# One of sixteen scan states weighted by C in transposed form on TensorE and ScalarE, and one more product with B on GpSimd, in an f32 selective-scan kernel

## The reference

```python
def step(h, inp):
    dt_t, B_t, C_t, x_t = inp
    dA = jnp.exp(dt_t[..., None] * A)
    dBx = dt_t[..., None] * B_t[:, None, :] * x_t[..., None]
    h = dA * h + dBx
    y = jnp.einsum('bdn,bn->bd', h, C_t)
    return (h, y)
...
return jnp.swapaxes(ys, 0, 1) + xc * D
```

## Time and profile before

| | |
|---|---|
| median of 3 runs | 16064.77 us (16052.41 to 16081.05) |
| the profiled execution | 16048.2 us, its span 16046.4 us |
| the gate's instructions, first to last | 2441.8 to 15980.0 us |
| busy share of the span | PE 88%, DVE 87%, POOL 81%, ACT 63% |
| granted TensorE clock | 0.932 of 2.4 GHz on the mean |

### The profile page before, as it was taken

The page is one execution under the profiler, slowest core; times in us unless marked ns, Lnnn a source line. Parts: engine busy times, 40 slices in busy tenths (PEclk is TensorE's granted clock), DMA queues, the critical chain, the costliest instruction groups (busy, mean ns, idle before and its releaser), DMA issues. The chain is left out here.

```text
span 16046.4 us, 144617 instructions
## 1 busy us (share of the span) xinstructions
PE 14080.0 (88%) x40704; PEld 5374.8 (33%) x40704; DVE 13972.3 (87%) x13537; ACT 10107.4 (63%) x14054; POOL 13048.9 (81%) x5650
## 2 busy tenths in 40 slices
PE   9999988888888888888888888888888888888887
PEld 3333333333333333333333333333333333333332
DVE  2222229999999999999999999999999999999998
ACT  2222226666666666766767667666666677666766
POOL 0000008999999999999999999999999999999997
PEclk9999998999999999999999999999999999999998
DMA  2111104444444545445455444554545454544545
GB/s 57 39 45 41 39 26 168 162 170 169 167 180 173 182 168 184 177 176 179 174 182 181 173 181 172 181 179 172 179 174 182 169 184 175 178 174 177 184 173 198
DMA packets 560175, 2505.16 MB, mean 156 GB/s; under 512 B 58919, under 2 KB 170879, under 8 KB 293264
## 3 DMA queue, kind: packets, MB, share of 16 engines
q1 hardware_dynamic: 548744, 2477.26, 43.7%
q10 hardware_dynamic: 10632, 18.65, 0.4%
HBM read 2325.11 MB, written 170.57 MB: 156 GB/s over the span
## 5 line engine op out<-in xcount | busy, mean ns | idle before, releaser
L811 POOL TENSOR_TENSOR hc<-h,c_all 128x1024 f32<-128x1024 f32 x4096 | 9526.8, 2358 | 490.3 <-DVE h L1178 460.5
L1048 PE MATMUL y_ps<-hc,ident 128*128 128x512 f32 x16392 | 8334.5, 660 | 1120.2 <-POOL hc L811 1119.9
L909 ACT ACTIVATE d_a<-dt,a_neg 128x512 f32<-128x512 f32 x8194 | 5598.2, 689 | 4045.1 <-DVE h L1178 4018.6
L1178 DVE TENSOR_TENSOR_SCAN h<-d_a,h,dbx_v 128x512 f32<-128x512 f32 x5456 | 6628.1, 1265 | 10.4 <-DVE dbx_v L1165 0.6
L1048 PEld LDWEIGHTS y_ps<-hc,ident 128*128 128x128 f32 x16392 | 3340.3, 210 | 6021.9 <-issue 4129.2
L1165 DVE TENSOR_TENSOR dbx_v<-dtx_ps,b_all 128x1024 f32<-128x1024 f32 x2816 | 3319.6, 1210 | 60.1 <-issue 25.2
L1178 DVE TENSOR_TENSOR_SCAN h<-d_a,h,dbx_p 128x512 f32<-128x512 f32 x2480 | 3029.4, 1263 | 10.4 <-issue 0.4
L800 POOL TENSOR_TENSOR dbx_p<-dtx,b_all 128x1024 f32<-128x1024 f32 x1280 | 3000.2, 2354 | 24.3 <-DVE h L1178 0.8
L495 POOL MEMSET ident_f<- 128x128 f32 x1 | 0.2, 204 | 2349.6 <-POOLq L46 2349.6
L289 PE MATMUL conv_ps<-image,w_taps 128*32 128x512 f32 x11520 | 1776.2, 594 | 0.0
L378 DVE RECIPROCAL k_inv<-k_nrm 128x4 f32<-128x4 f32 x256 | 45.5, 178 | 1750.0 <-ACT k_nrm L231 1750.0
(11 more groups left out here) (146 smaller groups left out, 9192.3 us busy)
## 6 DMA issues: line engine op xcount, KB each, us to landing
b_all<-bc_dram SPq DMA_DIRECT2D x1028, 1024.0 KB, 6.5
c_all<-bc_dram SPq DMA_DIRECT2D x1025, 1024.0 KB, 5.0
o_dram<-o_sb SPq DMA_DIRECT2D x257, 256.0 KB, 6.2
o_c<-o_dram SPq DMA_DIRECT2D x220, 256.0 KB
out<-r_c SPq DMA_DIRECT2D x220, 256.0 KB, 8.0
image<-in_x SPq DMA_DIRECT2D x91, 512.0 KB, 4.1
un<-un_dram SPq DMA_DIRECT2D x736, 34.0 KB
bc_dram<-low_bc SPq DMA_DIRECT2D x257, 64.0 KB, 4.7
```

What stands on the lines that cost most here:

```text
L811: nc.gpsimd.tensor_tensor(hc[:, n % HC], h[:, n], c_all[:, n // CG % 2, n % CG].unsqueeze(1).broadcast_to([128, 2, CH]), ALU.mult).then_in ...
L909: nc.scalar.activation(d_a[:, half], dt[:, p, half], ACT.Exp, scale=a_neg[:, half, n:n + 1]).then_inc(a_done, 1)
L1048: last = nc.tensor.matmul(y_ps[:, half], ident[:], hc[:, n % HC, half], start=False, stop=(n == S - 1))
L1178: nc.vector.tensor_tensor_scan(h[:, n, half], d_a[:, half], dbx, zero_col[:] if first else h[:, n, half, CH - 1:CH], ALU.mult, ALU.add).th ...
```

## The change

- State 9 (`TURNED`) is no longer multiplied with C by GpSimd. TensorE transposes its `h` in eight 128x128 blocks into `p_ps` (`turn`), ScalarE multiplies it on the way to SBUF with C as a scale per partition (`weigh_turned`, four activations of 128x256), and TensorE adds it to `y_ps` by eight matmuls with the identity, which turn it back (`add_turned`). C's row of the state comes as a column, by one more small DMA per chunk (`load_col`).
- GpSimd has 15 products with C in a chunk in place of 16, and six with B in place of five: `ON_POOL` gains state 5, VectorE makes ten.
- The orders of GpSimd, ScalarE, TensorE and VectorE within a chunk are new. `r_c` has one buffer in place of two, and small tiles are put together.

```diff
-ON_POOL = [7, 9, 11, 13, 15]
+ON_POOL = [5, 7, 9, 11, 13, 15]
+TURNED = 9
+WEIGHED = [n for n in range(S) if n != TURNED]
+WS = len(WEIGHED)
...
+            def load_col(p):
+
+                sp.dma_start(c_col[:, p], bc_dram[p, S + TURNED].rearrange("(j t) -> t j", t=128),
+                             allow_slow_non_contiguous=True).then_inc(col_in[p], 16)
...
                 after(pool, "scan", 2 * S * km + 2 * n + 2)
-                after(pool, "y_mm", S * km + n + 1 - HC)
+                run = WS * km + WEIGHED.index(n)
+                before = run - HC
+                after(pool, "y_mm", S * (before // WS) + WEIGHED[before % WS] + 1)
...
+            def weigh_turned(km, i, p):
+
+                after(act, f"turn_mm{i}", km + 1)
+                after(act, f"col_in{p}", 16 * (km // 2 + 1))
+                if km > 0:
+                    after(act, "y_mm", S * (km - 1) + TURNED + 1)
+                for j in (0, 1):
+                    last = nc.scalar.activation(hct[:, 2 * i + j], p_ps[:, 1 - i, 256 * j:256 * j + 256], ACT.Identity,
+                                                scale=c_col[:, p, 2 * i + j:2 * i + j + 1])
+                last.then_inc(turned[i], 1)
...
+            def turn(km, i):
+
+                after(pe, "scan", 2 * S * km + 2 * TURNED + 2)
+                if i == 0:
+                    after(pe, "o_copied", km + 1)
+                else:
+                    after(pe, "tail_copied", tails_before(km + 1))
+                for j in (0, 1):
+                    for half in range(2):
+                        c0 = (2 * i + j) * 128
+                        last = nc.tensor.transpose(p_ps[:, 1 - i, 256 * j + 128 * half:256 * j + 128 * half + 128],
+                                                   h[:, TURNED, half, c0:c0 + 128], ident[:])
+                last.then_inc(turn_mm[i], 1)
+
+            def add_turned(km):
+
+                after(pe, "turned0", km + 1)
+                after(pe, "turned1", km + 1)
+                for half in range(2):
+                    for j in range(SUB):
+                        last = nc.tensor.matmul(y_ps[:, half, 128 * j:128 * j + 128], hct[:, j, 128 * half:128 * half + 128],
+                                                ident[:], start=False, stop=False, skip_group_check=True)
+                last.then_inc(y_mm, 1)
```

More of the change, by code:

```diff
@@ L654, in phase_b @@
         share_set = stage("share_set")
+        col_in = [stage("col_in0"), stage("col_in1")]
+        turn_mm = [stage("turn_mm0"), stage("turn_mm1")]
+        turned = [stage("turned0"), stage("turned1")]
         def after(eng, name, runs):
@@ L751, in body @@
                 load_b(2, 1 - p)
-                after(sp, "hc_done", i + 3 * CG)
+                after(sp, "hc_done", i + 11)
                 load_c(0, 1 - p)
+                after(sp, "turned0", km)
+                after(sp, "turned1", km)
+                load_col(1 - p)
                 after(sp, "scan", 2 * S * km + 2 * S - 1)
@@ L780, in _ @@
             after(sp, "gm_in", 16 * (B - 1))
+            for p in range(2):
+                after(sp, f"col_in{p}", 16 * (B * NCH // 2 + 1 - p))
             for s in range(2):
@@ L804, in weigh_out @@
             def weigh_out(km, n):
-                if n % CG == 0:
+                if n == min(m for m in WEIGHED if m // CG == n // CG):
                     g = n // CG
@@ L955, in body @@
                 decay(km, 7, 1, p)
+                rows(km)
                 decay(km, 8, 0, p)
                 decay(km, 8, 1, p)
-                rows(km)
+                softplus(km, q)
                 decay(km, 9, 0, p)
@@ L1003, in inner @@
                 after(pe, f"un_in{p}", 32 * loads)
+                after(pe, f"turned{half}", km)
                 if half == 0:
@@ L1044, in add_state @@
             def add_state(km, n):
-                after(pe, "hc_done", S * km + n + 1)
+                run = WS * km + WEIGHED.index(n)
+                after(pe, "hc_done", run + 1)
                 for half in range(2):
-                    last = nc.tensor.matmul(y_ps[:, half], ident[:], hc[:, n % HC, half], start=False,
+                    last = nc.tensor.matmul(y_ps[:, half], ident[:], hc[:, run % HC, half], start=False,
                                             stop=(n == S - 1))
                 last.then_inc(y_mm, 1)
+            def turn(km, i):
[18 more added lines that the diff above has]
+                last.then_inc(y_mm, 1)
             def share_out(b, km):
+                after(pe, "turned1", km)
                 after(pe, "st_done", 3 * b)
@@ L1176, in run_scan @@
                 after(dve, "a_done", 2 * S * km + 2 * n + half + 1)
-                after(dve, "hc_done", S * km - S + n + 1)
+                if n == TURNED:
+                    after(dve, "turn_mm0", km)
+                    after(dve, "turn_mm1", km)
+                else:
+                    after(dve, "hc_done", WS * (km - 1) + WEIGHED.index(n) + 1)
                 nc.vector.tensor_tensor_scan(h[:, n, half], d_a[:, half], dbx,
@@ L1280, in body @@
                     aggregate(b, km)
+                run_scan(km, 12, 0, first)
+                run_scan(km, 12, 1, first)
+                weigh(km, 14)
+                run_scan(km, 13, 0, first)
+                run_scan(km, 13, 1, first)
+                run_scan(km, 14, 0, first)
+                run_scan(km, 14, 1, first)
                 run_scan(km, 15, 0, first)
```

102 lines of the change are left out of this document (47 added, 55 removed).

## The result

The changed kernel took 15977 us (median of 4 runs, 15960 to 15986) against 16068 us for the kernel before: ratio 0.9942, 95% interval 0.9930 to 0.9954. It is faster by 0.6%; 16120 had been predicted, and a slowdown as the likeliest case. A second series gave 0.9934 (0.9920 to 0.9947).

A forecast was written before the change was run, and what follows sets the result against it. VectorE's stream was taken to bound the kernel now. After the change, chunks at 52.1, 52.86 and 54.26 us average 52.84 against 52.60: +0.24 x 257 = +62 us on 16048, 16110 to 16127, said as 16120; range 15880 to 16290.

The forecast's parts named there:

- a slowdown as the likeliest case: The loop across engines, lengthened by falls of TensorE's clock, sets the time: +0.24 us per chunk, 16050 to 16210, chance 0.43.
- VectorE's bound: VectorE's own instructions and waits in a chunk of the changed kernel: 52.1 us, 0.5 under the present 52.6.
- direct waits: On VectorE: +0.12 us for a scan right behind its product, +0.22 for a product right behind its scan.
- silu of z: On ScalarE, behind the gate and ahead of the Exp of state 5: VectorE waits 0.74 us for that state's scan.
- GpSimd, TensorE's and ScalarE's additions: GpSimd 22 instructions, 50.8 us; TensorE's transposes 1.0, turned adding 1.8 to 2.5; ScalarE's four activations 1.6; TensorE's and ScalarE's hidden.
- The loop gate, skip, state 0, projection, state 1, product 5: From gate through TensorE, GpSimd's products, x matmul and silu to the next gate: 51.16 us at full clock.
- long stretch: TensorE at clock 0.56 over 7 us, losing 3.1 us: loop 54.26 us, taken for 1.5 chunks in 10.
- short stretch: TensorE at clock 0.76 over 7 us, losing 1.7 us: loop 52.86 us, taken for 5.5 chunks in 10.
- the 4 us of idle move right ahead of skip, 0, projection, 1: TensorE idles from about 2.5 us before the gate to the skip; clock falls then land in the loop behind the gate.
- Rival 1: TensorE's clock does not fall there, or only behind state 1; VectorE's bound holds: -155 us, 15900, chance 0.34.
- point of decision: Clock loss from which the loop, not VectorE's bound, sets the period: 0.9 us (52.1 - 51.16).
- The image boundaries: Once-per-image work, other 0.3 us of the mean chunk: left as it is, no change in cost forecast.

## Why the prediction was wrong, point by point

- **VectorE's bound, a mis-sized term.** 52.1 us predicted, 51.56 measured. The direct waits came as sized (8022.73 to 8025.31, a pair of scans ahead of product 3, is 2.58 again), but one was left out: scan 4 directly behind product 4 (8032.35 to 8033.60, +0.12). The mis-sized term is the silu of z: the scan of state 5 starts 6.00 us behind the gate, 0.27 late and not 0.74, and 0.12 of that is the direct wait. The table load does not wait for the gate; it starts at 8032.04, the gate ends at 8032.43. Worth 0.47 us a chunk, some 100 us in all. Some periods of the runs in which the loop has slack are shorter still, 51.37 us.
- **GpSimd, TensorE's and ScalarE's additions.** 22 instructions of 2.31 us hold. Eight transposes have 1664 records, 253.0 us: 1.2 us for the 1.0 taken, and not the 2.2 that the prediction also named; the turned adding starts at 8010.40 and the next at 8012.26, 1.86 for 1.8; the four activations are 0.41 us of busy time each for 0.4. All hidden, as placed.
- **The loop gate, skip, state 0, projection, state 1, product 5.** It exists: product 5 starts 8.90 us behind the gate for the 8.64 predicted, and in the runs with the long idle ahead of the skip it sets the time (54.6 us for the 54.26 of the long stretch; 334 us back when the projection leaves it). At full clock it was put 0.4 us too short, 51.16 for 51.56, and the 0.9 us of slack that the prediction gave it are not there: a short stretch behind the gate, 1.7 us of loss, costs 1.7 (54.9 for 53.2).
- **The failed step: "the 4 us of idle move right ahead of skip, 0, projection, 1", and the fall of the clock behind it, with 3 chunks in 10 undisturbed.** In the changed kernel the idle is in two pieces. The first, 1.3 us between the x and z matmuls, waits for the silu of x; the prediction named it nowhere. At 228 of 240 gates the clock falls behind that piece, on the z matmuls and states 14 and 15, and the second piece, 3.0 us ahead of the skip where the clock is full, shrinks to 1.3 us. There the short stretch fits into the slack ahead of the gate, and only the long one costs, 1.65 us. 162 of 240 periods are as short as without a fall, not 3 in 10. Behind the gate, where the prediction put the falls, are 12.
- **What each of the two was worth, and where luck was in it.** The mean chunk is 52.17 us for the 52.84 forecast. 0.54 of the difference is the quiet chunk. The falls cost 0.61 in the mean for the 0.74 forecast, so by size they are 0.13 of it. That these two figures lie near each other is chance: the forecast's falls were at another place, and where they do lie there, with the z matmuls last, they cost 3 us in most chunks. The direction needed both: with 52.1 for the quiet chunk and the falls as measured, a chunk would be 52.7 us, no less than before.
- **Rival 1** is what happened, in part. Its condition, no fall behind the gate, holds at 228 of 240 gates. Where it gave -155 us from VectorE's bound, the 162 quiet chunks are 1.1 us below the mean of before, the 69 long ones above it. Its point of decision, a loss of 0.9 us, was wrong with the loop's size: the loop decides from the first loss on.
- **The image boundaries**, left "as it is", cost 51 us more. The aggregate's new place is part of the change and the prediction did not follow it: while VectorE stands, ScalarE's activations of the turned state stand, and TensorE's order behind them. That explains 14 us in one order and 24 in another, as the runs with the aggregate moved back show; most of the rest is the gate waiting for `y_ps` there.

## What to carry to other kernels

When work moves in an engine's order, list all of its idle pieces in the new order with their ends, not only the longest: which of them the clock falls behind decides whether the stretch at half clock hits work that something waits for. The cure that worked was not to keep the clock up but to take 2 to 3 us of waiting out of the loop that crosses the engine; adding work to keep the engine busy cost more than it gave back. A step that leaves one loop lands in another: the late projection freed product 5 and held up scan 7. Before a slow run is blamed on the path one has in mind, see which wait in its long chunks is the long one. Follow once-per-image work too when it moves past a new dependence.

## What was not expected of the hardware

- Behind an idle of 1.3 us between matmuls of 49 rows the granted clock falls to its lower level ahead of 228 of 240 gates of the changed kernel. With 1.7 us of matmuls in the gap it falls there at none of 240.
- Stretches at half clock in the changed kernel came in two lengths, 3.4 and 6.9 us, but for 11 of 288, so that the chunk periods come in heaps (51.55, 53.2, 54.9) with little between.
- An activation table load began 0.39 us before the end of the gate for which the activation behind it waited: the wait did not stand ahead of the load. The load ahead of the silu of x (8073.39) did start only behind the x matmul, after 0.53 us of idle.
